# Sorted rows of a two-layer mixture kernel: 16-bit parts scattered and loaded by transposing DMAs, normalisation in paired steps, the choice of experts taken from logits

## The chip, the cores and the metric

One core of one Trainium2 chip runs the kernel. The metric is device microseconds of one execution, the median over several runs.

## The reference

2048 rows of 128 numbers (8 sequences of 256) go through two residual layers. Layer 0 pools each row over its sequence by a masked softmax, then adds a gated sum over 8 experts (128 to 512 to 128, tanh-gelu); every expert is applied to every row. Layer 1 first applies an adapter and a normalisation that depend on the sequence's language, then a mixture in which each row uses its two best experts:

```python
x = hidden_states + adapted                      # adapter: relu(x W1 + b1) W2 + b2 of the language
normed = (x - mean) * jax.lax.rsqrt(var + LN_EPS)
x2 = normed * gamma[language_ids] + beta[language_ids]
...
xn = (x2 - mu) * jax.lax.rsqrt(var + LN_EPS) * gamma + beta
probs = jax.nn.softmax(jnp.einsum('bld,de->ble', xn, gate_w), axis=-1)
w, idx = jax.lax.top_k(probs, TOP_K)             # TOP_K = 2
w = w / jnp.sum(w, axis=-1, keepdims=True)
h = jax.nn.gelu(jnp.einsum('bld,edh->eblh', xn, w1) + b1, approximate=False)
out_e = jnp.einsum('eblh,ehd->ebld', h, w2) + b2
output = einsum(cw, out_e) + x2                  # cw holds the two weights of each row
```

## The kernel before

The rows form four groups of 512. Layer 0 runs all groups **dense**: a unit is one expert, one group and 128 of the 512 hidden values, and there are 160 dense units, of which 128 come first (layer 0). In layer 1 the groups 0 to 2 are **sorted**: each row is written twice, to the places of its two experts, in a table `sorted_in` in DRAM, and 19 tiles of 256 sorted rows are read from it, each with the weights of its expert. A tile is two units, so there are 38 tile units. Group 3 runs dense in layer 1, the last 32 units. Then the results of the tiles, written to `sorted_out`, have to be gathered and weighed for groups 0 to 2.

Every matmul unit has a first part (into the hidden bank, three matmuls with 16-bit high and low parts of both factors, L589 to L591 or L566 to L568), a gelu on ScalarE (L675, L669), a split of its result in a high part `h16` (ScalarE L687, or VectorE L689) and a low part `l16` (VectorE L699), and a second part (L640 for the units in full precision, L651 to L653, or L628 to L630 for tiles). The second part stands about four units behind the first in TensorE's queue.

Between the dense units stands, for each group g, the chain `mid(g)`: `h` (pe_h L1319) and `act_h` (L1332), `xa` (L1341, L1342), statistics (L1350, L1355), a power on GpSimd for the reciprocal root (`rstd`, L1369), `n1` (L1378), scale and shift (L1392, L1400: on GpSimd, but on VectorE for group 2), the same again without scale for `n2` (L1416, held in `n2A`), transposes of both (`x2T` L1424, `nT` L1431), `xn` (ScalarE L1441), the logits `lg` (L1454), their exponentials (ScalarE L1465), the choice of two experts (`top`, VectorE L1481 to L1539), the ranks (`pe_rank` L1601 to L1605, `rank` L1617 to L1629) and eight scatters on GpSimd (L1721). After the scatters of group 2 a tile is loaded (L1759), transposed on TensorE (L1766), scaled by ScalarE (`act_x` L1775), and split by VectorE (L1782) and GpSimd (L1786).

The order on each engine is a queue sorted by hand-given positions: `at(queue, position, function)`, where the position counts units. `M0[g]` is 70, 86, 102 and 134; a table `AT`, with exceptions per group in `PLACE`, gives the offset of each step from `M0[g]`. The first tile unit has position 128. A wait blocks everything behind it on its engine. Three of these lines: a step of a chain on TensorE, the tile loads (three buffers), and the wait of the first gather for all tile results:

```python
at("pe", mpos[("nT", g)], pe_nT)
...
at("sp", p - 1 if i < NX else tpos(i - NX) + 0.5, sp_in)
...
pool.wait_ge(t_ys[z], 16 * ((NTL + 1 - z) // 2))
```

## Time and profile before

| | us |
|---|---|
| median of 3 runs | 386.85 (386.45 to 387.94) |
| the profiled execution: its own time | 388.65 |
| its span | 386.8 |
| first tile unit starts on TensorE | 255.48 |
| first dense unit of group 3 starts | 323.80 |

The profiled execution is one of its own and took 1.8 us more than the median. Its span is what the trace covers. Starts are counted from the span's begin. PE is TensorE's matmul, PEld its weight load, DVE VectorE, ACT ScalarE, POOL GpSimd, SP SyncE.

### The profile page before, as it was taken

Reading aid. Unit: us, or ns where it says so; the run is one execution under the profiler, and the core shown is the slowest. Engines: PE = TensorE matmul, PEld = TensorE weight load, DVE = VectorE, ACT = ScalarE, POOL = GpSimd, SP = SyncE. Lnnn points to the kernel's source line nnn. Section 1 sums busy time; section 2 is a strip of 40 time slices with the busy share of each in tenths; the row PEclk is TensorE's granted clock in tenths of the full one; section 3 lists DMA queues with packets and bytes.
Section 4 is the critical chain, followed back from the end, with each engine's and each line's share of the span. In section 5 each row is a group of like instructions: output and inputs, shape, how many; then the busy total and the mean of one; then the engine's idle time right before and its main releaser. Section 6 shows DMA issues by size and latency. Waiting matters only on the chain.

```text
span 386.8 us, 7491 instructions
## 1 busy us (share of the span) xinstructions
PE 353.4 (91%) x2092; PEld 203.7 (53%) x2093; DVE 263.0 (68%) x760; ACT 256.2 (66%) x451; POOL 226.6 (59%) x211
## 2 busy tenths in 40 slices
PE   8997999999999999969879786979999899999982
PEld 6765554444444454544445342437978787444430
DVE  0467748877649986757977757317798985367661
ACT  2465477877867657948794472649889898756650
POOL 6499999100026888717555786733378460287884
PEclk9999999999999999989998896969999999999998
DMA  7749922620066763642540111121324225631221
GB/s 204 256 104 371 399 89 67 179 43 0 9 169 140 144 128 72 151 93 70 100 120 17 58 43 35 47 71 44 109 76 128 67 69 90 157 94 42 66 57 54
DMA packets 47456, 40.94 MB, mean 106 GB/s; under 512 B 6978, under 2 KB 41522, under 8 KB 47290
## 3 DMA queue, kind: packets, MB, share of 16 engines
q1 hardware_dynamic: 44632, 36.12, 34.7%
q0 software_dynamic: 1760, 3.71, 3.3%
q10 hardware_dynamic: 1026, 0.65, 0.5%
q8 instruction: 18, 0.29, 0.3%
q14 instruction: 20, 0.16, 0.1%
HBM read 28.80 MB, written 11.67 MB: 105 GB/s over the span
## 4 chain that ended last, share of the span: by engine, by line
PE 57%; DVE 13%; POOL 12%; issue 11%; DMA 2%; ACT 2%; POOLq 0%; SPq 0%; DVEq 0%; ACTq 0%
PE bank L640 12%; POOL whl L1820 6%; PE bank L589 6%; PE bank L591 6%; PE bank L590 6%; PE bank L651 3%; PE bank L652 3%; PE bank L653 3%; POOL acc L767 3%; DVE l L699 2%; PE bank L566 2%; PE bank L1037 1%; PE bank L1341 1%; PE bank L1090 1%; PE bank L568 1%
## 5 line engine op out<-in xcount | busy, mean ns | idle before, releaser
L675 ACT ACTIVATE h<-bank,b1f 128x512 f32<-128x512 f32 x160 | 105.2, 686 | 84.1 <-PE bank L640 61.3
L699 DVE SCALAR_TENSOR_TENSOR l<-h 128x512 f16<-128x512 f32 x118 | 93.3, 794 | 20.7 <-ACT h L687 16.0
L767 POOL TENSOR_TENSOR acc<-acc,tmp 128x512 f32<-128x512 f32 x47 | 69.9, 1487 | 62.4 <-DVE tmp L740 60.0
L640 PE MATMUL bank<-h,w 128*128 128x512 f32 x160 | 83.3, 603 | 0.0
L687 ACT ACTIVATE h<-h 128x512 f16<-128x512 f32 x108 | 67.9, 629 | 2.1
L589 PE MATMUL bank<-xh,whl 128*128 128x512 f16 x128 | 49.3, 385 | 0.0
L591 PE MATMUL bank<-xh,whl 128*128 128x512 f16 x128 | 49.2, 385 | 0.0
L590 PE MATMUL bank<-xl,whl 128*128 128x512 f16 x128 | 49.2, 385 | 0.0
L1820 POOL DMA_INDIRECT whl<-sorted_out,idx x24 | 24.1, 1006 | 24.6 <-DMA sorted_out<-yo 18.3
L640 PEld LDWEIGHTS bank<-h,w 128*128 128x128 f32 x160 | 30.7, 195 | 11.6 <-issue 0.6
L669 ACT ACTIVATE h<-bank,b1f 128x256 f32<-128x256 f32 x76 | 31.4, 474 | 4.8 <-PE bank L568 2.6
L1786 POOL TENSOR_TENSOR xtl<-wraw,xth 128x256 f16<-128x256 f32 x19 | 15.7, 828 | 30.2 <-DVE xth L1782 30.2
L1721 POOL DMA_INDIRECT sorted_in<-n2A,idx x24 | 26.1, 1089 | 8.5 <-issue 5.5
L740 DVE SCALAR_TENSOR_TENSOR tmp<-bank,b2T,Gs 128x512 f32<-128x512 f32 x28 | 20.9, 746 | 13.1 <-PE bank L653 10.0
L628 PE MATMUL bank<-first,h 128*128 x152 | 28.0, 219 | 1.8 <-DVE l L699 1.6
L629 PE MATMUL bank<-first,h 128*128 x152 | 27.6, 220 | 0.0
L630 PE MATMUL bank<-first,l 128*128 x152 | 27.5, 219 | 0.0
L651 PE MATMUL bank<-h,w 128*128 128x512 f16 x64 | 25.2, 394 | 1.3 <-DVE l L699 1.2
L652 PE MATMUL bank<-h,w 128*128 128x512 f16 x64 | 25.3, 395 | 0.0
L653 PE MATMUL bank<-l,w 128*128 128x512 f16 x64 | 25.2, 394 | 0.0
L589 PEld LDWEIGHTS bank<-xh,whl 128*128 128x128 f16 x128 | 13.2, 103 | 21.6 <-issue 15.2
L566 PE MATMUL bank<-xth,first 128*128 128x256 f16 x76 | 21.4, 281 | 1.8 <-issue 0.9
(225 smaller groups left out, 710.1 us busy)
## 6 DMA issues: line engine op xcount, KB each, us to landing
Gs<-gates SPq DMA_DIRECT2D x40, 256.0 KB, 5.1
wraw<-in_w SPq DMA_DIRECT2D x16, 512.0 KB, 3.8
sorted_in<-zer SPq DMA_DIRECT2D x14, 448.0 KB, 6.7
wraw<-sorted_in SPq DMA_DIRECT2D x19, 128.0 KB, 2.2
sorted_out<-yo SPq DMA_DIRECT2D x19, 128.0 KB, 1.8
first<-in_xtm SPq DMA_DIRECT2D x1, 1024.0 KB, 8.9
mg<-in_gbc SPq DMA_DIRECT2D x8, 128.0 KB
w<-in_w SPq DMA_DIRECT2D x8, 128.0 KB, 2.8
```

The source lines that it names most:

```text
L589: pe.matmul(o[:, :], w_h, a, start=True, stop=False)
L590: pe.matmul(o[:, :], w_h, b_, start=False, stop=False)
L591: pe.matmul(o[:, :], w_l, a, start=False, stop=True).then_inc(s_m1, 1)
L640: pe.matmul(o[:, :], w2[:, e, j * 128:j * 128 + 128], h32[:, u % NH, :], start=(c == 0), stop=(c == 3))\
L651: pe.matmul(o[:, :], w_h, a, start=(c == 0), stop=False)
L652: pe.matmul(o[:, :], w_l, a, start=False, stop=False)
L653: pe.matmul(o[:, :], w_h, b_, start=False, stop=(c == 3)).then_inc(s_m2, 1)
L675: act.activation(h32[:, u % NH, :], bank[u % 4][:, :], ACT.Gelu if layer else ACT.Gelu_apprx_tanh, bias=b1f[layer][:, e * 4 + c:e * 4 + c ...
L687: eng.activation(dst, h32[:, u % NH, :], ACT.Copy, scale=HS).then_inc(s_hia, 1)
L699: dve.scalar_tensor_tensor(l16[:, slot(u), :], h32[:, u % NH, :], HS, h16[:, slot(u), :], ALU.mult, ALU.subtract).then_inc(s_lo, 1)
L767: pool.tensor_tensor(a, a, tmp[:, i % NTMP, :], ALU.add).then_inc(s_acc, 1)
L1820: pool.indirect_dma_start(yg[:, n, :], None, scy, bass.IndirectOffsetOnAxis(idx2[:, k, i:i + 1], 0))\
```

## The change

1. The normalised rows `n2` of groups 0 to 2 now carry scale and shift, are split once into two 16-bit parts (`act_rows` on ScalarE, `pool_rows` on GpSimd) and scattered as one row of 512 bytes. A tile is loaded by two DMAs with `transpose=True`, straight into `xt`, whose halves are the high and the low part; the transposes on TensorE and the steps `act_x`, `dve_x` and `pool_x` are gone. The load of tile i waits for the first part of tile i-3.
2. Subtract-and-scale and multiply-and-shift are paired in four VectorE steps (`s1`, `s2`, `n2a`, `n2`); those with the mean go ahead of the reciprocal root. Scale and shift leave GpSimd.
3. The experts are chosen from the logits; one power on GpSimd (`pool_e`) gives the exponential of the difference of the two best. The weights follow in `weights()`, and the ranks wait for the choice alone (`m_oh`).
4. The last addition of layer 0 of each group is VectorE's.
5. New tables `MID` and `LATE` place the steps.

```diff
@@ positions
-PLACE = [
-    {"lg": 17.6, "d": 17.2, "exp": 17.4, "top": 17.8, "rank": 24.5, "scatter": 9.7},
...
+MID = {
+    "h": 1.6, "act_h": 1.5, "xa": 3.1, "stats": 3.6, "rstd": 4.4, "s1": 4.6, "s2": 5.6, "stats2": 6.7, "rstd2": 7.6,
...
+PLACE = [LATE, MID, MID, {"s1": 5.5, "s2": 7.5, "n2a": 10.2, "lg": 17.6, "d": 17.2, "top": 17.8, "e": 19.0, "w": 21.5}]
@@ additions
-            at("pool", pos + AT["add"], add(i, kind, v))
+            if i + 1 in done0.values():
+                at("dve", pos + 0.05, add(i, kind, v))
+            else:
+                at("pool", pos + AT["add"], add(i, kind, v))
@@ normalisation
-            def dve_n1(dve):
...
+            def dve_s1(dve):
...
+                for i in range(4):
+                    last = dve.scalar_tensor_tensor(n1[:, i * 128:i * 128 + 128], o[:, i * 128:i * 128 + 128], mv[:, 0, i, 0:1],
+                                                    gbc[:, 2 * g + i // 2, 0:D], ALU.subtract, ALU.mult)
+                last.then_inc(m_n1, 1)
...
+            def act_rows(act):
+                act.wait_ge(m_n2, g + 1)
+                act.activation(rows_of(0), n2f[:, :].rearrange("p (t d) -> p t d", t=4), ACT.Copy).then_inc(m_xh, 1)
+
+            def pool_rows(pool):
+                pool.wait_ge(m_xh, g + 1)
+                pool.tensor_tensor(rows_of(1), n2f[:, :].rearrange("p (t d) -> p t d", t=4), rows_of(0), ALU.subtract)\
+                    .then_inc(m_xs, 1)
@@ choice
-            def act_exp(act):
-                act.wait_ge(m_d, g + 1)
-                act.activation(ex[:, :, :], lg[:, :, :], ACT.Exp).then_inc(m_e, 1)
+            def pool_e(pool):
+                pool.wait_ge(m_dd, g + 1)
+                if g:
+                    pool.wait_ge(m_cw, g)
+                pool.tensor_tensor(ee[:, :], base[:, :], dd[:, :], ALU.pow).then_inc(m_e, 1)
...
@@ ranks
-                pe.wait_ge(m_cw, g + 1)
+                pe.wait_ge(m_oh, g + 1)
@@ tiles
                 if i >= NX:
-                    sp.wait_ge(t_tr, i - NX + 1)
+                    sp.wait_ge(s_m1, US + 2 * (i - NX) + 2)
                 r = sp.value_load(tei[0:1, 2, i:i + 1], min_val=0, max_val=E * CAP)
-                sp.dma_start(xr[:, i % NX, :, :], scx[bass.ds(r, TS), :].rearrange("(z p) d -> p z d", p=128))\
-                    .then_inc(t_xr[i % NX], 16)
...
+                for k in range(2):
+                    sp.dma_start(xt[:, i % NX, k * TS:k * TS + TS], scx[bass.ds(r, TS), k * D:k * D + D], transpose=True)\
+                        .then_inc(t_xr[i % NX], 16)
...
-            at("sp", p - 1 if i < NX else tpos(i - NX) + 0.5, sp_in)
-            at("pe", mpos[("t", i)], pe_t)
-            at("act", p + 0.1, act_x)
-            at("dve", p + AT["tdve"], dve_x)
-            at("pool", p + 0.3, pool_x)
+            at("sp", p - 1 if i < NX else US + 2 * (i - NX) + 2.3, sp_in)
```

How rows move, at three places. First ScalarE before the adapter step of group 1 (`hTs`): before, the exponentials and two loads of activation tables stand right ahead of it.

```order
L675 ACTIVATE h<-bank,b1f 128x512
L1465 ACT_TABLE_LOAD
L1465 ACTIVATE ex<-lg 128x32
L687 ACTIVATE h<-h 128x512
L675 ACT_TABLE_LOAD
L675 ACTIVATE h<-bank,b1f 128x512
L1332 ACTIVATE hTs<-bank,cb 32x256 x2
```

The same place now:

```order
L891 ACTIVATE first<-wraw 128x1024
L675 ACTIVATE h<-bank,b1f 128x512
L754 ACTIVATE tmp<-bank 128x512
L1335 ACTIVATE hTs<-bank,cb 32x256 x2
L687 ACTIVATE h<-h 128x512
```

The exponentials and both table loads are gone, and on TensorE two units now stand between `h` and `xa` of group 1, where there was none.

Second VectorE between the logits of group 2 and the ranks, before:

```order
L1481 TENSOR_REDUCE c<-ex 128x4
L740 SCALAR_TENSOR_TENSOR tmp<-bank,b2T,Gs 128x512
L1485 RECIPROCAL c<-c 128x4
L1489 TENSOR_TENSOR pr<-ex,c 128x32
L1494 MAX mx<-pr 128x8 x4
L1500 MAX_INDEX ix<-mx,pr 128x8 x4
...
L699 SCALAR_TENSOR_TENSOR l<-h 128x512
...
L1528 TENSOR_TENSOR cumb<-cumb,OB 128x8 x4
L1533 TENSOR_TENSOR oh<-oh,wk 128x32 x2
L1539 TENSOR_TENSOR cw<-oh 128x32
```

and now (the rank matmul waits for `cumb`):

```order
L1474 COPY lg<-bank 128x32
L1498 MAX mx<-lg 128x8 x4
L1503 TENSOR_TENSOR dd<-mx 128x4
L1505 MAX_INDEX ix<-mx,lg 128x8 x4
L1510 CAST ixf<-ix 128x32
L1515 TENSOR_TENSOR oh<-iota,ixf 128x32 x2
L1524 COPY OH<-oh 128x2x32
L1528 TENSOR_TENSOR OB<-oh 128x32
L699 SCALAR_TENSOR_TENSOR l<-h 128x512
L1533 TENSOR_TENSOR cumb<-cumb,OB 128x8 x4
```

Sum, reciprocals, products and the weights no longer stand ahead of the ranks. On TensorE the ranks of group 2 stood after 119 first parts and now stand after 117.

Third SyncE, the load of one tile in the middle of the tile stage, before:

```order
L1797 DMA sorted_out<-yo 128x2x128
L1758 TENSOR_LOAD tei
L1758 ISA x2
L1759 ISA
L1759 DMA wraw<-sorted_in 128x2x128
```

and now:

```order
L1805 DMA sorted_out<-yo 128x2x128
L1791 TENSOR_LOAD tei
L1791 ISA x2
L1793 ISA
L1793 DMA_TRANSPOSE xt<-sorted_in 128x256
L1793 ISA
L1793 DMA_TRANSPOSE xt<-sorted_in 128x256
```

One load became two transposing ones.

## Rows read from the trace of the kernel before

**Rows 1.** Page, part 1: busy us, share of the span, instructions.

```profile
PE 353.4 (91%) x2092; PEld 203.7 (53%) x2093; DVE 263.0 (68%) x760; ACT 256.2 (66%) x451; POOL 226.6 (59%) x211
```

**Rows 2.** Waits of PE: line waited for, us in total, times, longest us.

```profile
PE bank L1341 <- ACT hTs L1332: 5.2, 2, 2.9
PE bank L1601 <- issue: 4.8, 1, 4.8
PE bank L1431 <- DVE n2A L1416: 2.1, 2, 2.0
PE bank L1766 <- DMA wraw<-sorted_in: 1.9, 2, 1.2
```

**Rows 3.** Windows: us, busy of PE, PEld, DVE, ACT, POOL; PEclk, DMA, GB/s.

```profile
235.50:241.00 5.50, 5.46 (x15) 2.20 (x16) 3.67 (x16) 1.32 (x2) 2.87 (x4) 0.55 0.07 24
...
255.40:261.00 5.60, 5.52 (x18) 2.85 (x19) 0.32 (x2) 2.37 (x5) 1.89 (x2) 0.51 0.17 50
261.00:324.00 63.00, 59.74 (x700) 50.94 (x699) 53.52 (x139) 55.81 (x125) 32.63 (x34) 1.00 0.29 81
323.80:381.00 57.20, 54.33 (x257) 26.60 (x254) 33.73 (x54) 33.58 (x54) 37.34 (x35) 1.00 0.35 80
```

**Rows 4.** Timeline of PE, dense units up to the first tile: start, us.

```profile
163.99 1.05 PE L1319 MATMUL bank<-acc,cw 128*32 128x256 f32 x4
...
174.33 1.02 PE L640 MATMUL bank<-h,w 128*128 128x512 f32 x2
...
177.13 1.02 PE L640 MATMUL bank<-h,w 128*128 128x512 f32 x2
...
192.42 0.60 PE L1431 MATMUL bank<-ident,n2A 128*128 128x128 f32 x4
...
195.65 0.95 PE L1454 MATMUL bank<-gw,xn 128*128 128x8 f32 x8
...
196.54 1.05 PE L1319 MATMUL bank<-acc,cw 128*32 128x256 f32 x4
...
235.54 0.18 PE L1601 MATMUL bank<-OB,triu 128*128 128x32 bf16 x1 [4.82 <-issue]
...
251.96 0.41 PE L1766 MATMUL bank<-ident,wraw 128*128 128x128 f32 x2 [1.19 <-DMA wraw<-sorted_in]
...
255.48 0.39 PE L566 MATMUL bank<-xth,first 128*128 128x256 f16 x1 [0.55 <-POOL xtl L1786]
```

**Rows 5.** Timeline of PE at full clock: the adapter of group 3.

```profile
272.39 0.44 PE L1341 MATMUL bank<-ident,acc 128*128 128x128 f32 x2
...
274.23 0.27 PE L566 MATMUL bank<-xth,first 128*128 128x256 f16 x1
```

**Rows 6.** ACT: table loads by form, and the adapter step of group 2.

```profile
L1465 ACT ACT_TABLE_LOAD x3 | 3.8, 1283 | 0.1
...
201.16 0.80 ACT L1332 ACTIVATE hTs<-bank,cb 32x256 f32<-32x256 f32 x2
```

**Rows 7.** Timeline of POOL, the last scatter; then of DVE, one step.

```profile
246.46 0.96 POOL L1721 DMA_INDIRECT sorted_in<-n2A,idx  x1 [0.30 <-issue]
...
215.67 2.96 DVE L1416 TENSOR_SCALAR n2A<-x,mv,rs 128x128 f32<-128x128 f32 x4 [0.38 <-POOL rs L1369]
```

**Rows 8.** Tile stage: ACT step L1775 by form, then two starts on PE.

```profile
L1775 ACT ACTIVATE wraw<-bank,fgs 128x256 f32<-128x256 f32 x17 | 9.7, 569 | 1.8 <-PE bank L1766 1.7
...
318.09 0.28 PE L566 MATMUL bank<-xth,first 128*128 128x256 f16 x1 [0.18 <-issue]
...
323.80 0.38 PE L589 MATMUL bank<-xbh,first 128*128 128x512 f16 x1
```

**Rows 9.** Page, part 6, DMA issues: KB each, us to landing.

```profile
Gs<-gates SPq DMA_DIRECT2D x40, 256.0 KB, 5.1
...
wraw<-sorted_in SPq DMA_DIRECT2D x19, 128.0 KB, 2.2
```

**Rows 10.** Page, part 5: the low parts on DVE, busy us, mean ns.

```profile
L699 DVE SCALAR_TENSOR_TENSOR l<-h 128x512 f16<-128x512 f32 x118 | 93.3, 794 | 20.7 <-ACT h L687 16.0
```

More of the change, by code:

```diff
@@ L314, in build_adaln_ffn @@
         s_w16 = sem("s_w16")
-        s_w2b = sem("s_w2b")
+        s_w2b = [sem(f"s_w2b{e}") for e in range(E)]
         s_w2f = sem("s_w2f")
@@ L384, in build_adaln_ffn @@
         m_e = sem("m_e")
+        m_dd = sem("m_dd")
         m_cw = sem("m_cw")
@@ L512, in tpos @@
             return max(US - 0.4 + 0.05 * i, US + 2 * i - 5 + AT["tile"])
-        for i in range(NTL):
-            misc.append((tpos(i), ("t", i), (t_x32, i + 1)))
         for g in range(GA):
@@ L1380, in dve_n1 @@
-                last.then_inc(m_n1, 1)
-            def scale(eng):
-                eng.wait_ge(m_n1, g + 1)
-                if g == 0:
-                    eng.wait_ge(ld["lang"], 16 * 4 * B)
-                else:
-                    eng.wait_ge(m_x2T, g)
-                    eng.wait_ge(m_n2, g)
-                for i in range(2):
-                    b = 2 * g + i
-                    v3 = n1[:, i * S:i * S + S].rearrange("p (t d) -> p t d", t=2)
-                    last = eng.tensor_tensor(v3, v3, gbc[:, b:b + 1, 0:D].to_broadcast([128, 2, D]), ALU.mult)
-                return last
@@ L1395, in shift @@
-            def shift(eng):
-                for i in range(2):
-                    b = 2 * g + i
-                    v3 = n1[:, i * S:i * S + S].rearrange("p (t d) -> p t d", t=2)
-                    o3 = x2[:, i * S:i * S + S].rearrange("p (t d) -> p t d", t=2)
-                    last = eng.tensor_tensor(o3, v3, gbc[:, b:b + 1, D:2 * D].to_broadcast([128, 2, D]), ALU.add)
+                    last = dve.scalar_tensor_tensor(x2[:, i * 128:i * 128 + 128], n1[:, i * 128:i * 128 + 128], rs[:, 0, i:i + 1],
+                                                    gbc[:, 2 * g + i // 2, D:2 * D], ALU.mult, ALU.add)
@@ L1430, in pe_nT @@
                 for i in range(4):
-                    last = pe.transpose(o[:, i * 128:i * 128 + 128], n2[:, i * 128:i * 128 + 128], ident[:, :])
+                    last = pe.transpose(o[:, i * 128:i * 128 + 128], n2f[:, i * 128:i * 128 + 128], ident[:, :])
                 last.then_inc(m_nT, 1)
@@ L1498, in _ @@
                 def _(dve):
+                    dve.tensor_tensor(dd[:, :], mx8[:, :, 1], mx8[:, :, 0], ALU.subtract).then_inc(m_dd, 1)
                     for i in range(4):
-                        dve.max_index(ix8[:, i, :], mx8[:, i, :], pr[:, i, :])
-                    return dve.tensor_tensor(c4[:, :, 3], mx8[:, :, 0], mx8[:, :, 1], ALU.add)
+                        last = dve.max_index(ix8[:, i, :], mx8[:, i, :], lg[:, i, :])
+                    return last
                 @part
                 def _(dve):
-                    dve.tensor_copy(ixf[:, :, :], ix8[:, :, :])
-                    return dve.reciprocal(c4[:, :, 4], c4[:, :, 3])
+                    return dve.tensor_copy(ixf[:, :, :], ix8[:, :, :])
                 @part
@@ L1527, in _, with weights, part @@
                         def _(dve, i=i):
-                            return dve.tensor_tensor(cumb[:, i + 1, :], cumb[:, i, :], OB[:, i, :], ALU.add)
+                            ins = dve.tensor_tensor(cumb[:, i + 1, :], cumb[:, i, :], OB[:, i, :], ALU.add)
+                            if i == 4 * g + 3:
+                                ins.then_inc(m_oh, 1)
+                            return ins
+                return parts
+            def weights():
+                parts = []
+                def part(fn):
+                    parts.append(fn)
                 @part
                 def _(dve):
+                    dve.wait_ge(m_oh, g + 1)
+                    dve.wait_ge(m_e, g + 1)
+                    return dve.tensor_scalar(c4[:, :, 0], ee[:, :], 1.0, None, ALU.add)
+                @part
+                def _(dve):
+                    return dve.reciprocal(wk[:, :, 0], c4[:, :, 0])
+                @part
+                def _(dve):
+                    return dve.tensor_tensor(wk[:, :, 1], ee[:, :], wk[:, :, 0], ALU.mult)
+                @part
+                def _(dve):
+                    if g:
+                        dve.wait_ge(m_cT, g)
+                    if g < GA:
+                        dve.tensor_copy(wA[:, sl, :], wk[:, :, :])
                     for k in range(2):
```

186 lines of the change are left out of this document (83 added, 103 removed), and 5 rows, old and new, of tables (LATE, MID).

## The prediction, made before the changed kernel ran

> **What bounds the kernel now.** I first read the page's busy shares: TensorE works 91% of the span, the others 59% to 68% [rows 1]. So time goes with TensorE, in its work, its waits, and its clock. The list of TensorE's waits names four that matter, and all lie in the chains between the dense units or at the first tile [rows 2]: `xa` waits for ScalarE's `hTs` (5.2 us in two waits), the ranks wait 4.8 us in one, `nT` waits for `n2A` (2.1 us), and the first tile transposes wait for their load (1.9 us). The windows show what follows such waits: after the wait for the ranks TensorE ran at a granted clock of 0.55, and over the first tile at 0.51, that is, near the lower level of 1.2 GHz, while most of the tile stage and the last dense stage stand at 1.00, 2.4 GHz [rows 3]. A wait here costs its length and then some slow matmuls.
>
> I split the span at three starts on TensorE: `h` of group 1 at 163.99, the first tile unit at 255.48 [rows 4], and the first dense unit of group 3 at 323.80 [rows 8]. Before 163.99 I cost the change at nothing: TensorE hardly waits there, and the earlier work is the same.
>
> *From 163.99 to 255.48, 91.5 us.* The order of the instructions puts 39 units here. At full clock two units take 177.13 - 174.33 = 2.80 us [rows 4], so 39 take 54.6. Between them stand two `h` (1.05 each), two `xa` (274.23 - 272.39 = 1.84 each, read at full clock [rows 5]), four `nT` and `x2T` (0.60), two `lg` (196.54 - 195.65 = 0.89) [rows 4], some 0.3 for ranks and `cT`, and three tile transposes of 0.41: 2.1 + 3.7 + 2.4 + 1.8 + 0.3 + 1.2 = 11.5. Work is 66.1 us, so **25.4 us are lost** in waits and at the low clock.
>
> *From 255.48 to 323.80, 68.3 us.* 38 tile units, 1.80 each, with group 3's chain among them. TensorE (59.7 of 63), ScalarE (55.8) and VectorE (53.5) are all nearly full from 261 on [rows 3].
>
> *From 323.80 on, 63.0 us.* TensorE is 54.3 of 57.2 us busy [rows 3]. The gathers of sorted results wait for the last tile, so both engines start from its end. The change leaves this part as it is. I take it as it stands.
>
> **The change part by part.** *No exponential on ScalarE.* A table load takes 1.28 us, and each of the three chains here has one for the exponential [rows 6] and, by the order, one more to return to gelu, right ahead of the `hTs` for which `xa` waits. They go, and two units (2.8 us) now stand between `h` and `xa` of group 1 as cover, as much as the 2.9 us of its longest wait [rows 2]. I take both `hTs` waits (5.2) to end. The work goes to a GpSimd power, and the ranks don't wait for it.
>
> *Paired steps.* From `xa` to `n2` the chain has two GpSimd roots. Today the subtract, and for group 2 also scale and shift on VectorE, follow the first; now `s1` and `n2a` run beside the roots, and GpSimd's scale and shift are gone. VectorE gets four steps of four instructions in place of two (of four for group 2). The worst such step took 2.96 us, begun just ahead of a scatter [rows 7]; I expect about 1.1 to 1.4 from its neighbours. Seven units cover the chain of group 2 before and after (9.8 us), with three low parts (0.79 each [rows 10]) and two larger steps in its queue. I leave 1.0 us of the 2.0 us wait.
>
> *Ranks from logits.* 4.8 us of wait [rows 2]. Ahead of the ranks the order drops the exponential's two table loads (2.6 us), the sum, two reciprocals, two products and the weights, eight small steps; but the cover shrinks to `x2T` and two units, 3.4 us. The steps left are about a dozen small ones and one low part, some 3.5 to 4.3 us. I leave 1.7 us over the three groups, against 4.8.
>
> *The additions on VectorE.* They shorten what `h` waits for, and TensorE doesn't wait there today (no such row in [rows 2]). Four units lie behind them: nothing. VectorE waits there for GpSimd's earlier additions, which precede the scatters: nothing, or some tenths.
>
> *The first tile.* From the ranks (235.54) to the arrival of the first tile (251.96) it took 16.4 us [rows 4]: ranks on VectorE, eight scatters on GpSimd up to 247.4 [rows 7], their landing, the load. These stay, with a second load to issue, some 17.7 us. TensorE now has 11 units (15.4 us) for it, not 9, and the first matmul follows the load at once: the 3.5 us from 251.96 to 255.48 for transposes, scaling and splits are gone. I leave 2.3 us of wait.
>
> Remaining waits are 1.0 + 1.7 + 2.3 = 5.0, and I add 1.0 for slow clock behind them. Bounds are 0 and today's 25.4. **Saving: 25.4 - 6.0 = 19.4, and 1.2 for the transposes, 20.6 us.**
>
> *The tile stage.* ScalarE loses 0.57 us per tile [rows 8], VectorE a cast, GpSimd a subtraction, TensorE two transposes. The trace shows such a stage already: from 318.09 to 323.80 no tile is left to be transposed or scaled, and four units take 5.71 us, 1.43 each [rows 8]. 38 units make 54.3. Group 3's chain on TensorE adds 1.05 + 1.84 + 1.2 + 0.89 + 0.1 = 5.1, and I add 2 for its steps on VectorE, where `n2` grows: 61.4 against 68.3. **Saving: 6.9 us.** Bounds: 0 (nothing of it shows), and 8.9 (without the 2).
>
> *The transposing loads.* No row shows one. A plain load of a tile, 128 KB, landed in 2.2 us; the slowest comparable transfer, the broadcast of gates, in 5.1 [rows 9]. Two loads per tile are issued four units, 5.7 us, ahead. Below, the pair costs no more than the plain load and is hidden; above, each takes 5.1 and they run one after another, 10.2 per tile, which makes 19 tiles 194 us. I take the pair at 2.2 to 3.5 us, nearest to the row that moves the same bytes from the same table, hidden behind a tile of 3.2 us.
>
> **The sum:** 388.65 - 20.6 - 6.9 = 361.15 for the profiled execution; it was 1.8 us above the median, so 359 us for the median.
>
> **The rivals.** *Transposing loads set the pace of the tile stage (slower).* If the pair of one tile takes 5.1 us, as one gate broadcast does, and pairs follow each other, 19 x 5.1 = 96.9 against 61.4 puts the time at 359 + 35.5 = 395. It speaks for it that the write side handles 2-byte elements; against it, that the plain load of the same bytes lands in 2.2 us. It decides above (61.4 + 27.5) / 19 = 4.7 us per pair: from there the kernel is slower. **Chance 0.20.** The Trainium skill ("VectorE: DVE Perf Modes", The three transpose paths) gives 1309 ns for one 128x128 bf16 transpose by DMA; a tile holds four, so the estimate by that page is 5.2 us per tile, 99.5 us for the stage and 397 us for the kernel. Another of its pages ("Advanced Engine Details and Errata", X-Bar Transpose) says that such DMAs are as fast as ordinary ones, which would hide them. No trace here shows which.
>
> *The chain of group 2 keeps its length.* From `h` at 196.54 to the ranks at 235.54 are 39.0 us [rows 4]; I have them at about 25. If the chain only loses its two table loads and half of its small steps, some 5 us, the wait moves to the ranks and the first tile, and 10 to 14 of the 20.6 us are not gained: 369 to 373. VectorE, with more steps and sharing its time with scatters as in [rows 7], speaks for it; that the loss today is made of short waits with slow clocks between speaks against it. **Chance 0.10.**
>
> *The tile stage stays as long as it is,* since loads come a little late or VectorE's additional steps fill it: 359 + 6.9 = 366 and up to 376 with pairs at 4 us. **Chance 0.10.**
>
> **How the numbers follow.** The forecast, 350 to 365, has 0.58; the rivals 0.20, 0.10, 0.10; 0.02 is no change. The likeliest gives 359. To leave out no more than 2 in 10 the range reaches over the second and third rival: 350 to 380. A measurement of this kernel tells a difference of about 0.5%, 2 us, from none. Faster 0.78, same 0.02, slower 0.20.
>
> **What would show it.** Waits of TensorE for `hTs` gone; for the ranks below 2 us; the first tile unit at about 235; granted clock near 1.0 from 200 to 235; 38 tile units in about 61 us, no wait of TensorE for `xt`; a transposing load landing in 3 us; 63 us behind the last tile unit. The prediction is wrong if TensorE waits for `xt` in most tiles, if the wait for the ranks stays above 3 us, or if the stage behind the tiles changes by over 2 us.

## The result and the profile after

The changed kernel took **396.44 us** (median of 4 runs, 395.67 to 399.28); the kernel before, beside it on the same chip, 386.65 us (386.04 to 387.94). The ratio is 1.025, with a 95% interval of 1.020 to 1.031: slower by 2.5%, where 359 us was forecast. In a later batch the same two kernels gave 394.90 and 388.66 us, a ratio of 1.014 (1.004 to 1.024). In the table below, "changed, again", "its stores on SyncE, split scatters", the first "16-bit transposes on TensorE" and "... split scatters" each have one slow execution, over 1.5% above their fastest, which counts in the median and not in the ratio; for the 16-bit transposes it is the profiled one, so that their last three columns are rough.

The profiled execution took 399.28 us, of which 397.6 is its span. Page, part 1, of the changed kernel, and the group of the tile loads in part 6:

```profile
PE 352.9 (89%) x2055; PEld 202.7 (51%) x2055; DVE 263.8 (66%) x761; ACT 240.5 (60%) x423; POOL 200.2 (50%) x184
...
xt<-sorted_in SPq DMA_TRANSPOSE x38, 2.3
```

TensorE is as busy as before in microseconds [rows 1], so the 10.8 us of span are, in sum, waiting. ScalarE lost 16 us of work and GpSimd 26, and neither shows in the time. A transposing load lands 2.3 us after its issue, the plain one took 2.2 [rows 9]: that was forecast. The waits of PE:

```profile
PE bank L566 <- DMA xt<-sorted_in: 19.2, 10, 4.1
PE bank L1447 <- DVE n2f L1420: 7.8, 3, 3.3
PE bank L1636 <- issue: 2.8, 2, 1.4
```

Against [rows 2]: the two waits for `hTs` (5.2 us) are gone, the wait for the ranks fell from 4.8 to 2.8 us. The waits of `nT` rose from 2.1 to 7.8, and a new one of 19.2 us stands in front of the tiles, though each load lands quickly. The timeline of PE places them:

```profile
161.88 0.63 PE L1447 MATMUL bank<-ident,n2f 128*128 128x128 f32 x4 [1.93 <-DVE n2f L1420]
...
170.97 0.83 PE L1322 MATMUL bank<-acc,cw 128*32 128x256 f32 x3
...
190.37 1.03 PE L1447 MATMUL bank<-ident,n2f 128*128 128x128 f32 x4 [3.35 <-DVE n2f L1420]
...
224.03 0.63 PE L1447 MATMUL bank<-ident,n2f 128*128 128x128 f32 x4 [2.51 <-DVE n2f L1420]
...
234.64 0.18 PE L1636 MATMUL bank<-OB,triu 128*128 128x32 bf16 x1 [1.41 <-issue]
...
254.33 0.28 PE L566 MATMUL bank<-xt,first 128*128 128x256 f16 x1 [4.05 <-DMA xt<-sorted_in]
...
334.43 0.38 PE L589 MATMUL bank<-xbh,first 128*128 128x512 f16 x1
```

The first tile unit comes at 254.33 (255.48 before), the first dense unit of group 3 at 334.43 (323.80). So up to the first tile 1.15 us were gained where 20.6 were forecast, the tile stage grew from 68.3 to 80.1 us where 61.4 was forecast, and what follows took 397.6 - 334.43 = 63.2 us against 63.0. The two questions are therefore why the tile stage waits for loads that land in 2.3 us, and what makes `n2f` late. Windows of the changed kernel, first around 34 us, then in the tile stage (columns as in [rows 3]):

```profile
34.00:38.00 4.00, 4.00 (x14) 2.93 (x14) 2.24 (x8) 0.00 (x0) 3.76 (x5) 0.50 0.95 301
38.00:42.00 4.00, 4.00 (x19) 2.58 (x18) 1.72 (x4) 1.90 (x4) 3.94 (x3) 0.72 1.03 416
...
261.00:332.40 71.40, 55.92 (x636) 48.32 (x635) 42.98 (x124) 46.09 (x101) 13.03 (x14) 0.94 0.30 78
```

The clock of 0.50, 1.2 GHz, at 34 us follows a wait of 2.1 us for `Gs` that the kernel before has too; it cost this execution some 4 us. A second profile of the same kernel (below) has 1.00 there, as others have or have not, whatever the kernel. I take it as a thing of single executions, and use the second profile where it matters.

### The profile page after: what moved, and what is told of

The parts are those of the page before. It is cut to its first block, busy times and chain, and to the rows that moved or that the text cites. A ratio compares the mean times of both kernels' runs of the same rounds, so it can differ in the third digit from the quotient of the medians.

```text
span 397.6 us, 7347 instructions
## 1 busy us (share of the span) xinstructions
PE 352.9 (89%) x2055; PEld 202.7 (51%) x2055; DVE 263.8 (66%) x761; ACT 240.5 (60%) x423; POOL 200.2 (50%) x184
## 4 chain that ended last, share of the span: by engine, by line
PE 36%; POOL 20%; issue 18%; DVE 11%; SPq 10%; DMA 3%; ACT 1%; POOLq 0%; DVEq 0%; ACTq 0%
PE bank L640 8%; POOL sorted_in L1756 7%; SPq L1793 7%; POOL whl L1824 6%; POOL acc L767 5%; PE bank L589 4%; PE bank L590 4%; PE bank L591 4%; PE bank L651 2%; PE bank L652 2%; PE bank L653 2%; DVE l L699 2%; DMA xt<-sorted_in 2%; PE bank L1093 2%; PE bank L1040 2%
## 5 line engine op out<-in xcount | busy, mean ns | idle before, releaser
L675 ACT ACTIVATE h<-bank,b1f 128x512 f32<-128x512 f32 x160 | 105.2, 687 | 83.1 <-PE bank L640 65.3
L699 DVE SCALAR_TENSOR_TENSOR l<-h 128x512 f16<-128x512 f32 x118 | 89.0, 762 | 19.7 <-ACT h L687 17.8
L767 POOL TENSOR_TENSOR acc<-acc,tmp 128x512 f32<-128x512 f32 x43 | 62.8, 1460 | 73.7 <-DVE tmp L740 60.6
L566 PE MATMUL bank<-xt,first 128*128 128x256 f16 x76 | 22.3, 293 | 19.5 <-DMA xt<-sorted_in 19.2
L1756 POOL DMA_INDIRECT sorted_in<-xs,idx x24 | 29.0, 1210 | 13.4 <-DVE idx L1664 7.4
L628 PE MATMUL bank<-first,h 128*128 x152 | 29.9, 229 | 0.0
L629 PE MATMUL bank<-first,h 128*128 x152 | 29.5, 229 | 0.0
L630 PE MATMUL bank<-first,l 128*128 x152 | 29.5, 228 | 0.0
L568 PE MATMUL bank<-xt,first 128*128 128x256 f16 x76 | 22.2, 292 | 0.0
```

What stands on the lines that cost most here:

```text
L675: act.activation(h32[:, u % NH, :], bank[u % 4][:, :], ACT.Gelu if layer else ACT.Gelu_apprx_tanh, bias=b1f[layer][:, e * 4 + c:e * 4 + c ...
L699: dve.scalar_tensor_tensor(l16[:, slot(u), :], h32[:, u % NH, :], HS, h16[:, slot(u), :], ALU.mult, ALU.subtract).then_inc(s_lo, 1)
L767: eng.tensor_tensor(a, a, tmp[:, i % NTMP, :], ALU.add).then_inc(s_acc, 1)
L1756: pool.indirect_dma_start(scx, bass.IndirectOffsetOnAxis(idx[:, k, i:i + 1], 0), xs[:, i, :], None)\
```

## The experiments

Times in us. "Tile" is the start of the first tile unit on TensorE, "stage" from there to the first dense unit of group 3, "rest" from there to the end of the span, all of the profiled execution; the ratio is to the kernel before in the same batch. The kernel before differs by up to 0.6% between batches (386.65 to 389.16), so ratios are compared across batches, and medians only within one. The two runs with plain loads and the two with small additions do not compute the reference; all others do.

| run | median | ratio (95%) | tile | stage | rest |
|---|---|---|---|---|---|
| before | 386.65 | 1 | 255.5 | 68.3 | 63.0 |
| changed | 396.44 | 1.025 (1.020 to 1.031) | 254.3 | 80.1 | 63.2 |
| changed, again | 394.90 | 1.014 (1.004 to 1.024) | 250.0 | 78.0 | 63.4 |
| one plain load | 375.00 | 0.969 (0.963 to 0.975) | 248.5 | 61.1 | 62.9 |
| two plain loads | 375.84 | 0.971 (0.966 to 0.976) | 250.2 | 61.5 | 63.2 |
| SyncE freed | 382.25 | 0.989 (0.984 to 0.995) | 250.4 | 63.3 | 65.3 |
| SyncE freed, again | 381.32 | 0.980 (0.976 to 0.985) | 252.4 | 64.7 | 64.0 |
| its stores on SyncE, split scatters | 390.41 | 1.004 (1.000 to 1.007) | 250.9 | 71.1 | 63.9 |
| 16-bit transposes on TensorE | 397.05 | 1.023 (1.015 to 1.030) | 255.6 | 77.3 | 63.2 |
| the same, copies in other order | 384.72 | 0.989 (0.984 to 0.994) | 252.6 | 66.2 | 63.4 |
| the same, late scatters | 383.45 | 0.990 (0.985 to 0.994) | 253.7 | 66.5 | 63.0 |
| SyncE freed, and late nT | 380.34 | 0.978 (0.974 to 0.982) | 250.3 | 63.2 | 65.3 |
| ... additions back on GpSimd | 383.59 | 0.986 (0.982 to 0.990) | 252.3 | 64.1 | 63.8 |
| ... late scatters | 378.97 | 0.977 (0.972 to 0.981) | 247.9 | 64.0 | 64.1 |
| ... split scatters | 382.71 | 0.980 (0.972 to 0.988) | 252.2 | 63.6 | 65.2 |
| ... late scatters, group 0 later | 376.96 | 0.972 (0.967 to 0.977) | 246.7 | 64.8 | 65.2 |
| ... small additions | 367.16 | 0.946 (0.940 to 0.951) | 237.3 | 63.4 | 65.5 |
| ... small additions, late scatters | 369.88 | 0.953 (0.948 to 0.959) | 238.9 | 65.2 | 64.0 |
| ... additions on VectorE | 372.80 | 0.964 (0.956 to 0.972) | 242.9 | 64.3 | 64.0 |
| ... the same, late scatters, group 0 later | **371.09** | 0.957 (0.952 to 0.962) | 242.3 | 63.6 | 64.0 |

### What the tile stage waits for

**One plain load.**

```diff
-                for k in range(2):
-                    sp.dma_start(xt[:, i % NX, k * TS:k * TS + TS], scx[bass.ds(r, TS), k * D:k * D + D], transpose=True)\
-                        .then_inc(t_xr[i % NX], 16)
+                sp.dma_start(xt[:, i % NX, :].rearrange("p (z d) -> p z d", z=2),
+                             scx[bass.ds(r, TS), :].rearrange("(z p) d -> p z d", p=128)).then_inc(t_xr[i % NX], 16)
```

> The changed kernel, but each tile is loaded by one ordinary DMA of 128x2x256 instead of two transposing ones; the rows arrive untransposed, so the tile results are other numbers, and all the rest of the work is the same. My theory: the transposing loads are what lengthened the tile stage from 68.3 to 80.1 us, and without them nothing in it is in short supply: tile stage 61 to 63 us, first tile unit at about 252.0 (one issue of 0.38 us and 2.2 us to land, against 2 x 1.15 and 2.3), and 396.4 - 18 - 2 = 376 us in all. Rival: the stage is long because of something else that the change brought (VectorE, ScalarE or the clock after a late start); then the stage stays above 75 us and the time above 390.

375.00 us, stage 61.1: as the theory said, and as the prediction had the stage (61.4) for loads that are hidden. The tiles start at 248.5 where I said 252.0; of the 5.8 us from 254.3 the early slow clock of the changed kernel's first execution is 4, and against its second profile (250.0) it is 1.5. Nothing else of the change lengthens the stage.

**Two plain loads.** The same edit with the loop over `k` kept and the two halves loaded apart.

> The changed kernel with two ordinary DMAs of 128x2x128 for each tile, in the place of the two transposing ones (rows untransposed, tile results other numbers). It keeps the number of loads, the small packets of 256 bytes and the places in the queue, and takes away only the transposing. Theory: what costs is that SyncE's queue is held 1.15 us by each transposing DMA; an ordinary one holds it 0.38, so a tile takes 2 x 0.38 + 0.74 + 0.37 + 0.47 = 2.3 us of SyncE, under the 3.3 us of TensorE: tile stage 61 to 63 us, within 1 us of the run with one ordinary load. Rival: the two short-packet loads themselves are slow (packets under 512 bytes); then the stage is at 70 us or more, and only the single load is fast.

375.84 us, stage 61.5. Neither the number of loads nor their small packets count; the rival falls.

**SyncE freed.** The transposing loads are back; the other DMAs of the stage are issued by GpSimd.

```diff
-            at("sp", US + 2 * i + 1 + LAG + 1.7, sp_out)
+            at("pool", US + 2 * i + 1 + LAG + 1.7, sp_out)
-            at("sp", US + 8.2 + 2.0 * e, load_w2b(e))
+            at("pool", US + 8.2 + 2.0 * e, load_w2b(e))
```

> The changed kernel with its transposing loads, but the other DMAs that SyncE issues in the tile stage (the stores to sorted_out and the eight loads of w2) are issued by GpSimd. Theory (SyncE's issue time is the limit): SyncE then needs 2 x 1.15 + 0.74 = 3.0 us for a tile instead of 3.9, less than TensorE's 3.3; TensorE's wait for the tiles falls from 19.2 us to under 5 and the stage from 80 to 62 to 66 us. Rival (the transposing transfer itself has a throughput of about one tile in 4 us, whoever issues what): stage stays at 78 to 82 us. A second rival: GpSimd's queue becomes late, and stores or scaled w2 are waited for.

Stage 63.3, and TensorE waits 4.7 us for tiles in all, 3.9 of it at the first. The same 38 transposing loads, landing as before in 2.4 us, are hidden once SyncE has nothing else to issue. The rest grew to 65.3 us, and to 64.0 in the second run of this kernel; that the stores come late behind GpSimd's other work is my reading and not shown. With 382.25 us this kernel is 1% faster than the one before, 2% in the second run. The row of its loads, in ns min/median/max, and its SyncE timeline:

```profile
L1793 SPq DMA_TRANSPOSE xt<-sorted_in x38: 1102/1160/2437, 246.7 to 308.4; - x38
...
246.69 59.11 SPq L1793 DMA_TRANSPOSE xt<-sorted_in  x36
```

The first row is the time for which an issue holds SyncE's queue, not the transfer. A plain load of the same half holds it 0.38 (the run with two plain loads). The second row shows that the queue is nearly full even here: 36 issues follow each other for 59 us with no wait for a buffer longer than 0.2, one tile every 3.4 us in the mean. The run was repeated as a base for the later batches.

> The kernel with stores and w2 loads on GpSimd again, as the base for the schedule variants, since the times of the kernel before differ by 0.5% between the chips of the earlier runs (387.19 and 389.16). Against the kernel before its ratio was 0.989; on the chip of the schedule variants the base should come to 381 to 384 if chips differ as these two medians do. Then late nT (380.34) and late scatters (378.97) gained 1 to 3 and 2 to 5 us.

**The changed kernel again**, for its SyncE queue and its clock.

> The changed kernel once more, unaltered, for a second profile of it and times beside the others. Its first profile lost 3.8 us between 26 and 42 us to a granted clock of 0.50 and 0.72, which the runs with ordinary loads or a freed SyncE did not show, though the instructions there are the same. If that is a thing of single executions, this profile has the clock at 1.00 there, a span of 393 to 395 us, and the first tile unit at about 250.5. If it belongs to the kernel, it shows again. Either way the tile stage should be 79 to 81 us.

The early clock was 1.00 and the first tile came at 250.0, as said; the span was 391.4 and the stage 78.0, 1.6 and 1 us under the lower ends of what I said. The timeline of SyncE in its tile stage:

```profile
272.58 2.42 SPq L1793 DMA_TRANSPOSE xt<-sorted_in  x2
275.04 0.58 SPq L1805 DMA_DIRECT2D sorted_out<-yo  x1
275.67 0.46 SPq L920 DMA_DIRECT2D w<-in_w  x1
276.96 2.41 SPq L1793 DMA_TRANSPOSE xt<-sorted_in  x2
279.42 0.79 SPq L1805 DMA_DIRECT2D sorted_out<-yo  x1
280.25 0.47 SPq L920 DMA_DIRECT2D w<-in_w  x1
281.60 1.13 SPq L1793 DMA_TRANSPOSE xt<-sorted_in  x1
```

One round is 276.96 - 272.58 = 4.38 us, the next 4.64, with no idle time in them: two transposing issues, a store, a `w2` load, and 0.8 to 0.9 us in which the queue reads the tile's address (L1791). In the whole stage SyncE waited 1.6 us. TensorE needs 61.1 / 19 = 3.2 us for a tile.

**Stores on SyncE, `w2` loads on GpSimd**, with the scatters split as below.

> As the run just named (split scatters), with the stores to sorted_out issued by SyncE again and only the w2 loads by GpSimd. SyncE then needs 2 x 1.15 + 0.74 + 0.37 = 3.4 us for a tile, about what TensorE takes (3.2 to 3.3). If the issue time is what counts, the stage is 1 to 4 us longer than with the stores on GpSimd (63), in waits of TensorE for the tiles; the stores land sooner, and the stage behind the last tile gets back the 2 us (65.3 against 63.2) that it had grown by. Sum: within 2 us of it, either way.

A miss in size: stage 71.1, not 64 to 67, and 390.41 us. Its SyncE timeline:

```profile
272.13 2.41 SPq L1795 DMA_TRANSPOSE xt<-sorted_in  x2
274.58 0.58 SPq L1807 DMA_DIRECT2D sorted_out<-yo  x1
275.87 2.39 SPq L1795 DMA_TRANSPOSE xt<-sorted_in  x2
278.31 0.58 SPq L1807 DMA_DIRECT2D sorted_out<-yo  x1
279.59 2.62 SPq L1795 DMA_TRANSPOSE xt<-sorted_in  x2
```

A round with a store is 3.74 us here. I had 3.4 by adding a plain store of 0.37; behind a transposing load it holds 0.58. In this stage SyncE waited 1.6 us in all, and the run with the same scatters and its stores on GpSimd has a stage of 63.6. That 19 x 3.74 gives just 71.1 is in part chance, since the first four rounds have no store (3.1 us) and some later ones take 4.0 to 4.65. The mean does not hang on such choices. From the first pair of transposing issues to the last, one tile takes 3.36 us of SyncE in the kernel with SyncE freed, 3.79 here and 4.18 in the changed kernel, and the stages of 63.3, 71.1 and 78.0 us are 18.8, 18.8 and 18.6 such rounds. So the stage follows the issuing queue at three loads of it; at the lowest TensorE, which needs 3.2, hardly waits any more (0.5 us behind the first tile).

**16-bit transposes on TensorE**: one plain load per tile, four matmuls with an identity, and copies of the two halves out of the bank by VectorE and ScalarE.

```diff
+                for k in range(2):
+                    for z in range(2):
+                        last = pe.matmul(o[:, k * TS + z * 128:k * TS + z * 128 + 128], xr[:, i % NX, z, k * D:k * D + D],
+                                         ident16[:, :], start=True, stop=True)
...
+            at("dve", p + 0.1, dve_x)
+            at("act", p + 0.3, act_x)
```

> The changed kernel with 16-bit rows scattered as it does, but loaded by one ordinary DMA a tile and transposed on TensorE by four 16-bit matmuls with an identity; VectorE copies the high halves and ScalarE the low halves out of the bank (256 columns each). Everything ahead of the tiles is that of the changed kernel. Expected: first tile unit at 253, tile stage 64 to 67 us (that of the kernel before was 68.3 with four passes of the transposes in 32 bits, and GpSimd's step), so about 396.4 - 14 - 1 = 381 us, 379 to 385. If the ScalarE copy of 0.57 us a tile was what set the 68.3 us before, the stage stays at 68 and the time comes to 383 to 385.

A miss: 397.05. ScalarE stood waiting for VectorE's copy, 14 times and 19.5 us between 262 and 325, with everything behind it. With ScalarE's copy first and VectorE's 0.6 units later:

> The changed kernel with ordinary loads and 16-bit transposes on TensorE, as in the run of 397.05 us, but ScalarE copies its half first and VectorE its half later (0.7 units behind), so that ScalarE does not stand waiting for VectorE's turn (19.5 us in 14 waits there). Expected: that order of copies was what made that run slow: tile stage 64 to 68 us and 381 to 386 us in all. If the stage stays above 72 us, the additional copies themselves fill ScalarE and VectorE.

384.72, stage 66.2, as said. And with the late scatters that are told below:

> Ordinary loads and 16-bit transposes on TensorE (384.72 us), with the late scatters. The chain part gains what it gained with transposing DMAs (about 2.5 us to the first tile unit), the tile stage stays at 66 and the tail at 63.4: 381 to 383 us, 2 to 4 above the one with transposing loads and a freed SyncE.

383.45, just above the 381 to 383 that I said, and a tile start of 253.7: the scatters gave nothing here that can be measured. With late scatters the transposing loads are the better way to transpose (0.977 against 0.990, and a stage of 64.0 against 66.5), provided that SyncE is free; without them the ratios (0.989 and 0.980 against 0.989) leave it open.

### What makes n2f late

All these stand on the kernel with SyncE freed.

**Late nT.** In groups 0 and 1 the steps from `nT` and `x2T` on stand 2.5 units later.

```diff
+LATER = ("nT", "xn", "lg", "d", "top", "rank", "e", "w", "x2T", "x2a", "cT")
+LATE.update({s: LATE[s] + 2.5 for s in LATER})
+MID1 = dict(MID)
+MID1.update({s: MID[s] + 2.5 for s in LATER})
+PLACE = [LATE, MID1, MID,
```

> The kernel in which GpSimd issues the stores and w2 loads (382.25 us), with one more change: in the chains of groups 0 and 1 the steps from the transposes nT and x2T on stand 2.5 units later on every engine. Theory A (the new tables place nT ahead of the time at which VectorE has n2f ready): TensorE's waits for n2f in groups 0 and 1 (1.97 and 3.35 us) and for the ranks there (1.41) are covered by units; group 2's 2.51 stays; the first tile unit moves from 250.4 to about 244 and the time to 376 (375 to 379). Rival B (VectorE's queue is full there, 9.8 of 10 us busy, and what is late is everything behind it): the waits reappear behind other lines, and the time stays at 381 to 383.

The waits of groups 0 and 1 for `n2f` went, and came back as 3.46 us at the ranks of group 1, 1.3 at those of group 0, 1.3 for a low part, and 3.06 at group 2's `nT`; the tiles start at 250.3 as before. Rival B holds for the start; the ratio of 0.978 is the base's (0.980 in its second batch).

**The last additions back on GpSimd.**

```diff
-            if i + 1 in done0.values():
-                at("dve", pos + 0.05, add(i, kind, v))
-            else:
-                at("pool", pos + AT["add"], add(i, kind, v))
+            at("pool", pos + AT["add"], add(i, kind, v))
```

> The same base (382.25 us), with the fourth part of the change undone: the last additions of layer 0 are GpSimd's again. If that part was neutral, as I costed it, the time is 381 to 383.5. If VectorE's additions are what made n2f late (0.7 us in its queue), the waits for n2f get 0.7 us shorter each and the time falls by 1 to 2 us. If they are worth something (GpSimd is then later at its powers and scatters, on which chain 2 and the first tile wait), the time rises by 1 to 4 us.

0.986 lies between the base's two ratios: no effect shown, as costed.

**Late scatters.** `LATE["scatter"] = 10.3`, and 10.15 for group 1: behind the next chain's powers.

> The same base (382.25 us), with the eight scatters of groups 0 and 1 placed behind the two powers of the next chain on GpSimd's queue (8 to 9 units later). Theory C (the scatters hold up the powers and share time with VectorE's steps): the step L1409 of group 1 falls from 2.87 to about 1.2 us and the 1.67 us wait for the power in group 2 goes, TensorE's waits for n2f in groups 1 and 2 fall from 3.35 and 2.51 to under 2 and 1, and the time by 2 to 4 us. Rival: it is GpSimd's additions (acc) that VectorE's long steps coincide with, the 2.87 us stays, and the time changes by less than 1 us, or rises as the last scatters of group 2 come later.

Waits for `n2f` in groups 1 and 2 fell to 1.78 and 0.97, and the start to 247.9. But the stretch did not go, it moved: now the step L1397 of groups 1 and 2 has an instruction of 1.36 us, and it runs beside one of GpSimd's additions. The part of theory C on the powers held, that on the scatters' sharing did not. In time the gain is small: 0.977 against 0.980 and 0.989.

**Split scatters.**

```diff
+LATE["scatter"] = 6.6
-                at("pool", RK[g] + after("scatter", g) + (0.9 * n if g < GA - 1 else 0.01 * n), scatter(g, 4 * g + n // 2, n % 2))
+                at("pool", RK[g] + after("scatter", g) + (0.9 * n if g < GA - 1 else 0.01 * n) + (4.5 if g == 1 and n > 3 else 0.0),
+                   scatter(g, 4 * g + n // 2, n % 2))
```

> As the run with late scatters (378.97), but with less crowding ahead of the last ones on GpSimd: group 0's eight scatters stand right behind the second power of the chain of group 1, and of group 1's eight four stand ahead of the first power of the chain of group 2 and four behind its second power (there all eight stood behind, and the last scatters of group 2 started 6.5 us after the ranks, behind them and two additions, instead of 3.2 us). Theory: the powers stay free and the last scatters start 2 to 4 us sooner after the ranks; the first tile unit at 244 to 246, 374 to 377 us. Rival: GpSimd has no room left between the chains (8.7 to 9.0 of 10 us busy there), the four early scatters delay the first power again, and the time stays at 378 to 380.

A miss, 382.71 beside a base of 381.32. The rival comes nearer, though it said 378 to 380: GpSimd is 8.7 us of 10 busy there. That this is the reason is not shown.

**Group 0 later by 1.5 units**, with the late scatters.

> The kernel with late scatters (378.97 us) and, for group 0 alone, the steps from nT and x2T on 1.5 units later. Nothing but the first tile depends on group 0 late, so its wait for n2f (1.93 us) and for the ranks should vanish behind units: 376 to 378 us. Rival: the wait only moves to the ranks of group 1 (3.46 us when both groups were moved by 2.5), and the time stays at 378 to 380.

376.96, as said: group 0's waits are gone. Against late scatters alone (0.977) the ratio of 0.972 is not clear of noise.

**Small additions.** GpSimd's additions of layer 0 cover 8 of 512 columns; most of the sum is left out.

```diff
+                n = 8 if eng is nc.gpsimd and i < max(done0.values()) else 512
+                a = acc[:, g * 512:g * 512 + n]
+                eng.tensor_tensor(a, a, tmp[:, i % NTMP, 0:n], ALU.add).then_inc(s_acc, 1)
```

> The kernel with stores and w2 loads on GpSimd (381 to 382 us), in which GpSimd's additions of layer 0 cover 8 of 512 columns (most of the sum is left out, all waits and orders stay). Theory D (VectorE's steps are held by GpSimd's additions and scatters): L1394 of group 0 falls from 3.16 to about 1.15 us, L1420 of group 0 from 2.14 to 1.15, the wait for n2f in group 0 (1.96) goes, and those of groups 1 and 2 fall by what the additions held, but the stretch beside the scatters (L1409, 2.87) stays at 1.6 or more. 3 to 6 us less in all. Rival E (the tables place nT too early whatever GpSimd does): the three waits for n2f stay above 6 us together.

367.16 us: by the ratios (0.946 against 0.980 and 0.989) 13 to 17 us less than the base, far more than the 3 to 6 that I said. VectorE's steps, ns min/median/max: first the kernel with SyncE freed (two steps), then this one (the same two):

```profile
L1394 DVE SCALAR_TENSOR_TENSOR x<-n,rs,mg x4: 340/848/1355, 147.9 to 150.7; 128x128 f32<-128x128 f32 x4
L1409 DVE SCALAR_TENSOR_TENSOR n<-x,mv,fgr x4: 340/345/2073, 182.1 to 184.6; 128x128 f32<-128x128 f32 x4
```

```profile
L1395 DVE SCALAR_TENSOR_TENSOR x<-n,rs,mg x16: 336/341/481, 149.1 to 264.3; 128x128 f32<-128x128 f32 x16
L1410 DVE SCALAR_TENSOR_TENSOR n<-x,mv,fgr x16: 340/347/472, 153.1 to 269.5; 128x128 f32<-128x128 f32 x16
```

An instruction of 0.34 us had taken 1.35 or 2.07. L1409 of group 1, which I had expected to stay long beside the scatters, is short too. The longest instruction and GpSimd in the kernel with SyncE freed, at the same times:

```profile
182.34 2.07 DVE L1409 SCALAR_TENSOR_TENSOR n<-x,mv,fgr 128x128 f32<-128x128 f32 x1
...
146.18 4.48 POOL L767 TENSOR_TENSOR acc<-acc,tmp 128x512 f32<-128x512 f32 x3
...
182.00 0.96 POOL L1756 DMA_INDIRECT sorted_in<-xs,idx  x1 [0.30 <-issue]
182.98 1.28 POOL L767 TENSOR_TENSOR acc<-acc,tmp 128x512 f32<-128x512 f32 x1
```

The long instructions of these steps outside the tile stage all end 0.15 us behind the end of an addition (182.34 + 2.07 = 184.41 against 182.98 + 1.28 = 184.26). This one began 0.64 us ahead of that addition, beside the last part of a scatter; 13 others that began beside a scatter took their usual time. What held it in those first 0.64 us stays open. The ranks' own steps are held too. The step on which the rank matmul waits, in group 1, first with SyncE freed, then in the run with additions on VectorE that is told below:

```profile
197.00 1.82 DVE L1533 TENSOR_TENSOR cumb<-cumb,OB 128x8 bf16<-128x8 bf16 x4
...
192.10 0.74 DVE L1535 TENSOR_TENSOR cumb<-cumb,OB 128x8 bf16<-128x8 bf16 x4
```

The waits of PE in the run with small additions:

```profile
PE bank L566 <- DMA xt<-sorted_in: 4.2, 4, 2.7
...
PE bank L1448 <- DVE n2f L1421: 1.6, 2, 1.0
```

**Small additions with late scatters.**

> The same small additions with the late scatters (378.97 us as it was). By theory D both causes are gone: all VectorE steps take 1.1 to 1.2 us, the waits for n2f fall to under 1.5 us together, the first tile unit comes at 241 to 244. By rival E more than 4 of the 4.7 us of waits for n2f are left.

369.88, the waits for `n2f` at 0.9, the start at 238.9. Theory D holds for the additions, and not for the scatters; rival E falls; with the additions small, late scatters only delay the last ones (5.4 us of wait at the first tile instead of 2.7).

**The additions on VectorE in whole**, from position 72 on; all is computed.

```diff
-            if i + 1 in done0.values():
-                at("dve", pos + 0.05, add(i, kind, v))
+            if i + 1 in done0.values() or (i < max(done0.values()) and pos > 72):
+                ap = max(pos + (0.05 if kind == "y" else AT["add"]), ap + 0.01)
+                at("dve", ap, add(i, kind, v))
```

> The kernel with stores and w2 loads on GpSimd (382.25 and 381.32 us), with the additions of layer 0 from position 72 on given to VectorE in whole (0.69 us each there, 1.3 to 1.7 on GpSimd). All is computed. Theory D: VectorE's steps are no longer held (all single instructions at about 0.34 us, as with the small additions), and GpSimd's powers wait for no addition; against it stand some 16 additions, 11 us more in VectorE's queue, which was 7.4 of 10 us busy with small additions. I expect the first tile unit at 240 to 244 and 371 to 375 us. Rival: VectorE's queue becomes what is late (low parts, n2f), the first tile unit stays at 248 or later, and the time at 380 or above.

372.80, start 242.9, as said, and the same two steps:

```profile
L1396 DVE SCALAR_TENSOR_TENSOR x<-n,rs,mg x4: 343/344/344, 150.4 to 151.2; 128x128 f32<-128x128 f32 x4
L1411 DVE SCALAR_TENSOR_TENSOR n<-x,mv,fgr x4: 344/346/353, 182.2 to 183.0; 128x128 f32<-128x128 f32 x4
```

Group 1's x step of that run on VectorE, and the scatter beside it on GpSimd (timelines):

```profile
178.06 1.13 DVE L1396 SCALAR_TENSOR_TENSOR x<-n,rs,mg 128x128 f32<-128x128 f32 x4
...
177.51 1.48 POOL L1758 DMA_INDIRECT sorted_in<-xs,idx  x1 [0.30 <-issue]
```

The scatter runs from before the step's begin to near its end, and the step takes its undisturbed 1.13 us. Still 4.8 us of waits for `n2f` are left in this run, against 7.8 in the base and 1.6 with small additions: VectorE's steps are no longer held, but its queue has 17 more additions to do, which is the likely reason and not tested apart. The additions themselves, in that run on either engine:

```profile
L767 POOL TENSOR_TENSOR acc<-acc,tmp x26: 1260/1284/1735, 114.7 to 363.0; 128x512 f32<-128x512 f32 x26
L767 DVE TENSOR_TENSOR acc<-acc,tmp x21: 680/691/718, 134.2 to 252.6; 128x512 f32<-128x512 f32 x21
```

**The same on the version with late scatters and group 0 later.**

> The same additions on VectorE in the version with late scatters and group 0 later (376.96 us). With small additions the late scatters were worth nothing or 2 us less than nothing (369.88 against 367.16), since the powers were not held up. So I expect this at 372 to 376 us, no better than the run on the base.

**371.09 us, 4.3% below the kernel before**: the best kernel here that computes the reference. It is 1.7 us below the run on the base; their intervals overlap, and I had said 372 to 376.

## Why the prediction was wrong, by its own steps

The forecast for the profiled execution was 361.15; the second profile took 393.11. The 32.0 us between them are 78.0 - 61.4 = 16.6 in the tile stage, 250.0 - 234.9 = 15.1 ahead of it, and 0.3 behind it.

**"The transposing loads ... hidden behind a tile of 3.2 us" failed.** I bounded the landing, and had that right (2.3 us). What I left out is how long an issue holds the queue that issues it: 1.15 us each and 2.4 a pair, beside 0.8 for the tile's address, 0.58 for a store and 0.47 for a `w2` load. SyncE's own row of one tile was never added up. The first rival named the right threshold, 4.7 us per pair above which the kernel is slower, and a time, 395, that came true by luck, since the mechanism was wrong: not the transfer sets the pace but the issue, and the stage lost half of what it assumed (16.6 against 35.5); the other half came from the chains. The third rival's upper end of 376 is a slip: pairs at 4 us make 19 x 4 - 61.4 = 14.6, so 374. The Trainium skill's 1309 ns for a 128x128 transpose by DMA ("VectorE: DVE Perf Modes", The three transpose paths) gave 5.2 us per tile; the freed queue took a tile's four every 3.4 us in the mean. Its other sentence, that such DMAs are as fast as ordinary ones ("Advanced Engine Details and Errata", X-Bar Transpose), agrees with the landing, 2.3 against 2.2 us, and says nothing of the issue.

**"The tile stage: 61.4" was right** for the work: 61.1 with plain loads.

**"I leave 1.0 us" for nT failed**: 7.8. I had seen a step of 2.96 us [rows 7], put it down to the scatter beside it and priced the new steps by their quiet neighbours. Right behind that scatter, in the kernel before, stands what the later runs point to:

```profile
217.00 1.27 POOL L767 TENSOR_TENSOR acc<-acc,tmp 128x512 f32<-128x512 f32 x1
```

The new steps read two operands from SBUF and stand where GpSimd adds. In the base four such stretches make (3.16 - 1.13) + (2.14 - 1.13) + (2.87 - 1.13) + (1.86 - 1.13) = 5.5 us. The additions also stand ahead of powers and scatters on GpSimd. With small additions `n2f` costs 1.6 us, the ranks 1.4, the first tile 2.7 and the clock 0.9: 6.6 where the prediction left 6.0, and the first tile comes at 237.3 where it said 235. So the working came out within some 2 us once this price was gone. How much of the 13 to 17 us is the hold itself and how much GpSimd's shorter queue is not separated; with the full sum on VectorE, which adds 17 x 0.69 = 12 us to it, 6 to 10 of them are had (0.964).

The rule was there to be read: by the Trainium skill ("SBUF — State Buffer", SBUF: two separate sides) VectorE and GpSimd share one pair of SBUF ports, taken as an exclusive lock by whichever starts first, also for a VectorE instruction with two SBUF inputs against a GpSimd one that reads SBUF. The trace agrees in size (a held instruction took 1.07 to 1.35 us and ended 0.15 us behind the addition; the longest, 2.07, is more than the lock of one addition explains by the profile, whose spans on GpSimd are rough) and in kind: beside additions held, beside scatters not, but for that one, and L1383, which reads its first operand from a bank, took 1.1 us for four at each place.

**"Ranks ... 1.7"**: 2.8, of 4.8; with small additions, where `cumb` takes its 0.75 us in every group, 1.4. **"First tile ... 2.3"**: 3.9, and 2.5 with a plain load. **"1.0 for slow clock"**: about 5 us between 150 and 250 in the second profile (the sum of one minus the granted clock over the 10 us windows), behind each of the waits for `n2f`.

**"Before 163.99 I cost the change at nothing" failed by 5 us**: up to unit 80 the two kernels agree (150.37 and 150.21), but unit 88 starts at 168.30 and not 163.25. Group 0's `n2f` and ranks lie there. Part of it is given back by group 1's adapter, which no longer waits.

**"ScalarE ... waits end", "the additions on VectorE: nothing" and "63.0 us behind the last tile"** were right (no `hTs` row; no effect shown; 63.2 to 63.4).

The second rival (the chain keeps its length) is the nearest for the part ahead of the tiles: it put 10 to 14 of the 20.6 us at risk, and 15.1 were missed.

## What to carry to other kernels

Add up the issuing queue like any engine: for each DMA the time for which its issue holds the queue (here 0.37 to 0.58 us plain, 1.15 transposing), for each address read from memory 0.7 to 0.9, per tile, and compare the sum with the tile's time; a landing time says nothing on it. When a step in the trace takes twice its neighbours' time, find what runs on GpSimd at that moment before taking the neighbours' price. An engine with spare time (GpSimd at 59%) can still be the wrong place for work: 17 additions moved from it to the busier VectorE made the kernel some 8 us faster.

## What the runs showed of the hardware

- A transposing DMA of 256 rows by 128 16-bit values held SyncE's queue 1.15 us (median of 38; 1.10 at least, now and then over 2), a plain one of the same bytes 0.38; a plain store right behind transposing loads took 0.58 where it takes 0.37 otherwise. Plain loads landed in 2.0 to 2.2 us, transposing ones in 2.3 to 2.5.
- Single VectorE instructions of 0.34 us with both tensors in SBUF took 1.07 to 2.07 us beside GpSimd's additions, and 0.34 beside scatters alone (12 of 12 in the run with additions on VectorE).
- A 128x512 addition took 0.69 us on VectorE and 1.28 to 1.74 on GpSimd.
- After the same wait of 2.1 us at 31 to 33 us of the span, the granted clock was 1.00 in some executions and 0.50 for 4 us in others, of the same kernel.
